# A graph layer on one core: five units of dense rows do their work in the list stage instead of in the last stage

## What is computed

```python
feats = [x]; cur = x                       # x: 100000 x 256, 25000 edges sorted by dst
for _ in range(3):
    cur = segment_sum(edge_weight[:, None] * cur[src], dst, 100000)
    feats.append(cur)
y = concat(feats) @ shared_weight + output_bias
out = layernorm(x + y)                     # over the 256 columns, no gain or bias
```

## Time and profile before

| | |
|---|---|
| three runs | 1513.71, 1514.54, 1518.88 us; median 1514.54 |
| the profiled execution | 1517.04 us, span 1515.3 us, TensorE's granted clock 0.973 of full |
| busy over the span | PE 91%, PE weight load 78%, DVE 74%, POOL 71%, ACT 69% |
| DMA | 286 GB/s over the span |

### The profile page before, as it was taken

One profiled execution on the slowest core, in us unless ns is written; L12 is line 12 of the kernel. 1 busy time (PEld: TensorE's weight loads), 2 busy tenths in 40 slices (PEclk: granted clock), 3 DMA queues, 4 the chain that ended last, 5 costly groups with the idle time before them and its releaser, 6 DMA issues. The chain is left out here.

```text
span 1515.3 us, 29727 instructions
## 1 busy us (share of the span) xinstructions
PE 1385.7 (91%) x7840; PEld 1178.2 (78%) x7840; DVE 1128.5 (74%) x3949; ACT 1044.5 (69%) x2940; POOL 1075.1 (71%) x1038
## 2 busy tenths in 40 slices
PE   6999999999999986659997999998999999889877
PEld 5888888888888874448886887787887777777766
DVE  7877777777777755897875476644998888878886
ACT  4767777777777752226775555554898888888887
POOL 4577777777777777565774677776377777777774
PEclk9999999999999998989999999999999999999998
DMA  7879988999888877338996688777999999999997
GB/s 251 266 252 308 310 299 285 312 301 306 286 280 285 275 204 172 134 95 288 321 320 249 154 246 246 207 198 170 342 376 334 350 339 338 330 337 329 362 413 258
DMA packets 218639, 421.55 MB, mean 278 GB/s; under 512 B 31863, under 2 KB 136874, under 8 KB 218474
## 3 DMA queue, kind: packets, MB, share of 16 engines
q1 hardware_dynamic: 167558, 323.81, 60.8%
q0 software_dynamic: 49920, 95.13, 22.3%
q10 hardware_dynamic: 996, 0.72, 0.2%
HBM read 230.99 MB, written 201.73 MB: 286 GB/s over the span
## 5 line engine op out<-in xcount | busy, mean ns | idle before, releaser
L1503 PE MATMUL ps_y<-w_sb,xT 128*128 128x256 f32 (+1 forms) x1832 | 478.0, 390 | 19.3 <-DVE y_ring L1836 19.3
L1503 PEld LDWEIGHTS ps_y<-w_sb,xT 128*128 128x128 f32 (+1 forms) x1832 | 338.7, 196 | 60.2 <-issue 16.2
L1216 ACT ACTIVATE o_ring<-y_ring,rstd 128x256 f32<-128x256 f32 (+1 forms) x782 | 349.8, 497 | 0.0
L1842 DVE BATCH_NORM_STATS2 stats<-y_ring 128x6 f32<-128x256 f32 (+1 forms) x782 | 292.6, 416 | 6.7
L1836 DVE TENSOR_TENSOR y_ring<-ps_y,bias 128x512 f32<-128x512 f32 x290 | 199.7, 689 | 127.6 <-PE ps_y L1503 105.9
L936 POOL DMA_INDIRECT rows_in<-in_x,gather_idx x200 | 203.1, 1015 | 85.8 <-issue 65.8
L936 POOL DMA_INDIRECT tails_found<-tail_keys,table_idx x200 | 201.4, 1007 | 72.8 <-issue 59.8
L936 POOL DMA_INDIRECT rows_in<-out_rows,early_node x184 | 191.7, 1042 | 77.9 <-issue 42.3
L1588 PE MATMUL ps_u<-w_sb,cT 128*128 128x256 f32 x788 | 209.2, 388 | 8.1 <-DVE u_out L2093 8.1
L940 POOL DMA_INDIRECT out_rows<-u_out,early_node x160 | 164.2, 1026 | 54.4 <-issue 36.0
L1203 ACT COPY xT<-ps_xT 128x512 f32<-128x512 f32 x252 | 144.0, 571 | 67.2 <-PE ps_xT L1492 67.1
(11 more groups left out here) (343 smaller groups left out, 2523.3 us busy)
## 6 DMA issues: line engine op xcount, KB each, us to landing
x_ring<-in_x SPq DMA_DIRECT2D x195, 512.0 KB, 5.8
out_rows<-o_ring SPq DMA_DIRECT2D x195, 512.0 KB
c_rows<-sums SPq DMA_DIRECT2D x49, 512.0 KB
u_rows<-u_out SPq DMA_DIRECT2D x49, 512.0 KB
keys_bc<-u_rows SPq DMA_DIRECT2D x20, 512.0 KB, 8.5
u_rows<-bias SPq DMA_DIRECT2D x15, 512.0 KB
listed<-u_rows SPq DMA_DIRECT2D x13, 512.0 KB
c_list_rows<-sums SPq DMA_DIRECT2D x11, 512.0 KB
```

The costliest lines, as they stand in the source:

```text
L1216: last = act.activation(o_ring[slot][0:rows, r * D:(r + 1) * D], y_ring[k][0:rows, r * D:(r + 1) * D], ACT.Copy, scale=rstd[k][0:rows, r:r ...
L1503: last = pe.matmul(y_bank[p][0:rows, r * D:(r + 1) * D], columns_in[p][:, q * P:q * P + rows], w_sb[:, c, :], start=c == 0, stop=c == KC - 1)
L1842: last = dve.bn_stats(stats[k][0:rows, r, :], y_ring[k][0:rows, r * D:(r + 1) * D])
```

## The change

Five units move from the last stage to the list stage. The five middle list steps get 2 units instead of 1; the last stage has 20 steps (d from 3 to 22), of which the last has 3 units, and the last step with the tail follows as step 23. All dense indices of the hops between move up by five, and nothing else of them. For all but the last unit of the list stage (14 of 15) the sum of squares is no longer made by VectorE: ScalarE squares the rows, two to a slot, with an accumulating ACTIVATE (`square_rows`, whose elementwise output goes into the unit's free `o_ring` rows), and the root waits for that. In the first hop the products of tiles 192 to 196 go to the buffers of `rows_in` (free by then), without the waits on stores and adds; the products of tiles 184 to 196 get their bias on VectorE, and POOL scatters them to the table without adding.

```diff
-    B_UNIT = LIST_UNIT + ONE * LIST_ALL + STEP
+    L_SIZES = (ONE,) * LIST0 + (PAIR,) * LIST_STEPS + (ONE,)
+    SQUARED = range(LIST_UNIT, LIST_UNIT + sum(L_SIZES) - 1)
+    B_UNIT = LIST_UNIT + sum(L_SIZES) + STEP
...
-    D_STEPS = REAL // Q
-    KEPT_STEPS = D_STEPS - 1
+    D_STEPS = 23
+    KEPT_STEPS = D_STEPS
...
-    D_SIZES = (0,) * E_STEPS + (FOUR,) * (D_STEPS - E_STEPS)
+    D_SIZES = (0,) * E_STEPS + (FOUR,) * (D_STEPS - E_STEPS - 1) + (STEP,)
...
-        rows_in = [sb(f"rows_in{k}", [P, D]) for k in range(Q)]
+        rows_all = sb("rows_in", [P, Q, D])
+        rows_in = [rows_all[:, k, :] for k in range(Q)]
+        U_LAST = Q * (A_STEPS - 1)
+        def u_rows(t):
+            return rows_all if t >= U_LAST else u_out
...
+                if t >= KEPT:
+                    scatter(u_dram[:, :], u_rows(t)[:, t % Q, :], index, tab_added[t // 2 % G])
+                else:
+                    pool.indirect_dma_start(u_dram[:, :], bass.IndirectOffsetOnAxis(ap=index, axis=0), u_rows(t)[:, t % Q, :], None,
+                                            bounds_check=bound, oob_is_err=False, compute_op=ALU.add).then_inc(tab_added[t // 2 % G], 16)
...
+            SQUARES_AT = {PAIR: {0: (-1, 0), 2: (-1, 1), 4: (0, 0), 6: (0, 1)}, ONE: {0: (-1, 0), 4: (-1, 1)}}
+            def square_rows(u, k, slot, turn, half):
+                act.wait_ge(y_copied, 2 * u + half + 1)
+                if half == 0:
+                    until(act, stored[slot], 16 * turn)
+                    act.wait_ge(std_ready, u - STEP + 1)
+                for r in (2 * half, 2 * half + 1):
+                    last = act.activation(o_ring[slot][:, r * D:(r + 1) * D], y_ring[k][:, r * D:(r + 1) * D], ACT.Square,
+                                          accum_out=squares[k][:, r:r + 1])
+                if half == 1:
+                    last.then_inc(unit_squared, 1)
             def roots(u, k, rows=P, tiles=RPP):
-                act.wait_ge(var_ready, u + 1)
+                if u in SQUARED:
+                    act.wait_ge(unit_squared, u - SQUARED.start + 1)
+                else:
+                    act.wait_ge(var_ready, measured_units(u) + 1)
...
             def unit_end(u, k):
-                dve.wait_ge(stats_ready, 2 * u + 2)
-                unit_squares(k)
+                if u not in SQUARED:
+                    dve.wait_ge(stats_ready, 2 * measured_units(u) + 2)
+                    unit_squares(k)
                 unit_inverse(u - 1, (k - 1) % STEP)
-                unit_variance(u, k)
+                if u not in SQUARED:
+                    unit_variance(u, k)
...
             def copy_u(j, k, stores):
                 dve.wait_ge(u_psum, 2 * j + 2)
+                if 2 * j < U_LAST:
+                    if k % G == 0:
+                        until(dve, u_stored[k // G], stores)
+                    until(dve, tab_added[j % G], tab_adds(j % G, 2 * j))
+                if 2 * j < KEPT:
+                    last = dve.tensor_copy(rows, ps_u[1][:, 0:n * D])
+                else:
+                    last = dve.tensor_tensor(rows, ps_u[1][:, 0:n * D], bias2[:, 0:n * D], ALU.add)
+                last.then_inc(u_copied, tiles_counted(2 * j + n - 1, n))
```

More of the change, by code:

```diff
@@ L852, in step_d @@
                     load_node_parts(d + 1)
-                for k in range(FOUR):
+                for k in range(dense[1]):
                     store_behind(dense, k)
@@ L1028, in _ @@
                 pool.wait_ge(gathered[q], 16 * A_STEPS)
+                limit(REAL * P)
+            for half in range(2):
+                pool.wait_ge(u_stored[half], 16 * A_STEPS)
+                limit(REAL * P)
+            for k in range(G):
+                pool.wait_ge(tab_added[k], tab_adds(k, REAL))
                 limit(REAL * P)
@@ L1233, in dense_slot @@
                         copy_xT(LAST_PAIR)
-                    for p in turns_at.get(2 * off + q, ()):
+                    done = TURNED_AT[units].get(q)
+                    for p in turns_at.get(2 * off + done, ()) if done is not None else ():
                         copy_xT(p)
@@ L1237, in dense_slot @@
                     copy_xT(2 * off + PAIR_AT[units][q])
+                if units in SQUARES_AT and q in SQUARES_AT[units] and off + SQUARES_AT[units][q][0] in SQUARED:
+                    u, slot, turn, k = unit_at(off + SQUARES_AT[units][q][0])
+                    square_rows(u, k, slot, turn, SQUARES_AT[units][q][1])
                 if q in ROOTS_AT[units] and has_rows(ROOTS_AT[units][q]):
```

59 lines of the change are left out of this document (32 added, 27 removed).

## The result

The changed kernel takes 1499.22 us (median of four runs, 1498.24 to 1499.65), the kernel before 1515.22 in the runs beside it (1513.71 to 1518.88). The ratio is 0.989, with a 95% interval of 0.9874 to 0.9906: 16 us, or 1.1%, faster. The forecast was 1503.8, with 1497.5 to 1513.5 as its range and 1499 to 1509 as the range of the forecast's own case. So the time lies inside both ranges, but at the lower edge of the second: the gain is half again as large as the 10.7 us of the forecast.

What follows compares the result with a forecast made beforehand. POOL's chain was taken as the bound in three places: first hop's end, list gathers, final scatters. -5.2 + 1 - 6.5 = -10.7 from the 1514.54 median gave 1503.8 us; range 1497.5 to 1513.5, own case 1499 to 1509 (0.62).

Steps and rivals of the forecast that it cites:

- rival 3: Last stage: the dense units are what it costs, so 26.5 us less there, 1484; chance 0.05.
- rival 1: Kernel's end: held by DMA, so only the first hop's -5.2 would stay, 1509; chance 0.12.
- 6 (no gain): Another wait takes the adds' place and the end is as before, 1514.5; chance 0.03.
- rival 2: List stage: VectorE, TensorE, ScalarE turn into a ring, pairs waiting for each; +7 to +15, 1510 to 1518; chance 0.11.
- Rival 4: List stage: TensorE falls to its lower clock and becomes the bound, five steps +31, 1534; chance 0.05.
- rival 5: ScalarE reloads its table between squares and roots, two loads a unit for 14 units, 1533; chance 0.02.
- First hop's end, -4.8 for the adds: Eight adds of 1.585 us ahead of the last look-up become plain transfers of 0.99: 4.8 us less.
- First hop's end, -0.4 for the BN_STATS: Ten us behind 597.85: one unit's BN_STATS (2 x 0.75) go from VectorE, partly gap filling, so 0.4 us less.
- List stage, +1: Five middle steps stay at POOL's 10.7 us; VectorE is held here and there by a pair: 1 us more.
- Last stage's end, -6.5: Last scatters at POOL's pace, the last 5.3 us earlier, end near 1508.4: -6.9, less 0.4 for DMA.
- The lower end of that term, -9.5: Last stage's end: the late rows come sooner as well, -9.5 us.
- The 0.4 taken off for DMA: Last 16 units' table rows load a step and a quarter earlier, into a stretch already at 413 GB/s: 0.4 us.

Runs made afterwards that it cites:

- the experiment: Only the first-hop part of the change (other buffers, bias on VectorE, plain scatters) in the kernel before: 1510.79 us against 1516.3, ratio 0.9965.
- The squares alone: In the kernel before, only the sums of squares of nine list units go to ScalarE: 1512.54 us against 1515.3, ratio 0.9974.

## Why the prediction held, and where it was short

**Direction and place: right; size: a third too small.** All three places named for the gain gave it, and the body of the last stage gave none to speak of. It is 617.4 to 621.0 us in the nine traces of the table, whether 84 or 79 units stand in it. Loading POOL lengthened it by the full net price, and a sixth unit moved gave nothing. That rules out rival 3 (1484). Rivals 1 (1509) and 6 (no gain) are out by the time, and rival 1 by the scatters too, which came at POOL's pace. The engines of the list stage did not form a ring (rival 2), as its gathers stayed at 1.333 us. ScalarE in the list stage of the change:

```profile
628.01 0.59 ACT L1229 COPY xT<-ps_xT 128x512 f32<-128x512 f32 x1
629.19 0.42 ACT L1239 ACTIVATE o_ring<-y_ring 128x256 f32<-128x256 f32 x1 [0.59 <-DVE y_ring L1882]
...
629.61 0.40 ACT L1239 ACTIVATE o_ring<-y_ring 128x256 f32<-128x256 f32 x1
...
630.13 0.30 ACT L1249 ACTIVATE std_all<-squares,eps 128x4 f32<-128x4 f32 x1
630.34 1.69 ACT L1258 ACTIVATE o_ring<-y_ring,rstd 128x256 f32<-128x256 f32 x4
```

and TensorE:

```profile
627.32 0.66 PE L1538 MATMUL ps_xT<-ident,x_ring 128*128 128x128 f32 x4 [1.05 <-ACT xT L1229]
627.81 1.89 PE L1549 MATMUL ps_y<-w_sb,xT 128*128 128x256 f32 x8
629.54 0.60 PE L1538 MATMUL ps_xT<-ident,x_ring 128*128 128x128 f32 x4
629.97 1.89 PE L1549 MATMUL ps_y<-w_sb,xT 128*128 128x256 f32 x8
```

The squares start 0.42 apart, as good as the 0.40 counted, and the eight products took 1.89. Rival 4 (the lower clock) did not come: the granted clock of the list stage was 1.00. Neither did rival 5. The trace of the change has one table load at the root's line, at 16.7 us of the span, though 56 squares now alternate with roots in the list stage:

```profile
L1249 ACT ACT_TABLE_LOAD x1 | 1.3, 1283 | 0.0
```

Here the Trainium skill's rule ("ScalarE: Activation LUTs", Table sets: the hidden batching unit), that a switch between sets costs a load, has nothing to act on.

**First hop's end, -4.8 for the adds: right**, 4.8 in the first pair of traces and 5.3 us by the median of the experiment.

**First hop's end, -0.4 for the BN_STATS: mis-sized, by some 2 us.** The step counted one unit's BN_STATS (1.5 us) in the ten us behind the landing, and held that they partly filled gaps. It is a unit and a half (2.2 us) that stands between the landing and the first list gather, and by the means over fourteen traces 2.3 us came off: nothing of it filled a gap. The squares alone gave 3.9 us by the medians (2.0 to 5.9). The piece is bounded by VectorE's order and not only by the landing at 597.85.

**List stage, +1: a little off.** It is -0.4 to -1.3 in the traces, and the two kinds of kernel overlap (56.8 to 57.8 before, 56.5 to 57.6 with the change's list). What was forecast of POOL's pace holds, with nothing to pay for a held VectorE.

**Last stage's end, -6.5: too small by some 2 in the traces.** The scatters came earlier behind the last gather as counted: 5.8 us in the first pair of traces and 5.0 in the second, against 5.3. Behind the last scatter's end I had left 10.8 us for the landing and the late loop; it was 12.4 before and is 9.5 now, so 2.9 came off where the forecast had 1.6. Before, the late rows of the table were asked for behind the last stores and VectorE waited 6.07 for them. Now three rows tell who is last (ScalarE's copy of the late columns, VectorE's sum, SP's load of the late rows):

```profile
1489.91 0.37 ACT L1516 COPY xT<-ps_xT 128x256 f32<-128x256 f32 x1 [9.19 <-PE ps_xT L1845]
...
1492.62 0.42 DVE L2826 TENSOR_TENSOR sums<-ps_y,keys_bc 128x256 f32<-128x256 f32 x1 [15.99 <-PE ps_y L1849]
...
1481.06 0.36 SPq L894 DMA_DIRECT2D keys_bc<-u_rows  x1
```

The load is issued at 1481.06, and the sum at 1492.62 waits for the product, thus for the late gather at 1486.99, which stands behind all scatters in POOL's queue. The bound went from SP's load to POOL's queue. The lower end of that term, -9.5, had named this ("the late rows come sooner as well"); the two pairs of traces give -8.6 and -8.0. The 0.4 taken off for DMA was not seen: the stretch's DMA share fell to 0.99 and then 0.50.

**Sum.** By the means over the traces, the terms of the forecast come to -5.0 for the adds, -2.3 for the BN_STATS, -0.6 in the list and -8.2 at the end: -16.1, beside the 16.0 of the medians. This agreement is closer than the readings allow. Stretches for which the forecast had nothing are some 2.5 us shorter as well (1.5 of it between the last list gather and the last gather of pointers, where no experiment looked for the cause), and the interval of the 16.0 us is 14.2 to 19.1. The medians also leave less for the end than the traces: 16.0 less 5.3 and 3.9 is 6.8, with some 3 us of uncertainty. So the rows show that the term of the BN_STATS was too small; that the end's was too, the traces say and the times leave open. That the forecast's own range still held the time, by 0.2 us, is in part luck: the errors of the terms all went one way.

## What to carry to other kernels

Where one engine's instructions fill a stage without a pause, work of the others can leave it and the stage stays as long (here 617 to 621 us with 84 units or with 79); ask then where the stage ends, since there the last step's work still stands between the last gather and the last store. Work moved into a stage must be counted on the engine that bounds it, together with what can leave that engine: here the same move was 1.1% faster with the squares on another engine, and 0.2% slower without. And before a piece of work is called a filler of gaps, count all instances of it between the event that releases the chain and the one that ends the stretch, and leave out those that stand ahead of the release.

## What was not expected of the hardware

- A memset of 0.236 us on POOL between two indirect transfers cost 0.07 to 0.08 us: it ran in part of the 0.30 us that pass between them. Some 300 register writes in the same place cost nothing, and taking them out left the pitch at 1.32 us.
- In 13 traces TensorE stood idle for 3.3 to 6.5 us ahead of the third hop's first products, and its clock fell to 0.5 behind that; in the one with 2.6 us of idle time it stayed at 1.00. The low clock goes with 0.9 to 2.5 us more in the stretch of waiting work behind it.
- POOL's counted loop with equal bounds (1 to 1) ran its body once: the second late gather at 1490.13.
